# Layer 0 attention: band addition, row maximum and negation in one VectorE instruction, exponential in place in SBUF

## The chip, the core and the metric

The kernel runs on one core of a Trainium2 chip. The metric is the time of one execution on the device in microseconds (us); lower is better. The engines are named as in the profile: PE (TensorE matmul), PEld (its weight load), DVE (VectorE), ACT (ScalarE), POOL (GpSimd) and SP (the engine that issues most DMAs). SBUF is the on-chip memory, PSUM the accumulator memory with 8 banks of 128 x 512 fp32.

## What is computed

A chain of four transformer-like layers on x of shape 8 x 512 x 128. Only the attention of Layer 0 is touched. It has 16 heads of 8 channels and a relative-position bias with two parts (content to position, position to content). Per head the scores are a 512 x 512 matrix: a product of query and key, plus bias terms that depend on a bucket of the distance between query and key (equal beyond 64 positions), then a softmax along each row, then a product with the values:

```
scores = (q @ k.T + c2p[bucket(i - j)] + p2c[bucket(j - i)]) * 1/sqrt(24)
probs  = softmax(scores, axis=-1)
out    = probs @ v          # then output projection, residual, layer norm
```

## The kernel before

Layer 0 has 8 batches x 16 heads = 128 heads (NBH), each cut into 4 blocks of 128 queries. A block, v = 4 * head + block, is one step: 128 partitions (queries) x 512 columns (keys). Every engine runs its own instruction stream, written out by hand as a loop over steps u; semaphores order the engines. The own bands and "frames" of the bias near the diagonal come back from DRAM (`scr`): `g_out` (DVE) sums them into GG, SP writes GG out (`write(n)`) and reads it back shifted (`read(n)`, into CD, three buffers).

One step goes through these stations:

- PE `scores(v)` (`l0_pe`, matmuls at L577 and L580) fills PSUM bank v % 3. It waits until the exponential of v - 3 has read that bank: `pe.wait_ge(s_ex, v - 2)`.
- DVE `add(v)` (L181) adds the block's own band, 192 or 256 columns wide, from CW to the scores in PSUM. CW has two buffers of 960 columns, one per head, filled by POOL's `own_band(n)` with two products of 192 and 768 columns.
- DVE `most(v)` (L193) takes the negated maximum of each row of 512 into MX. In every second step `g_out` stands between `add` and `most`.
- ACT `exp(v)` (L167) reads PSUM, adds MX and writes the exponential to the probability buffer PB[v % 3]. It waits for `t_mm`, the transposes of v - 3.
- PE `p_tr(v)` (L335) transposes the four 128x128 pieces of PB, in loop step u = v + 4, after `scores(u)`.
- ACT `p_out(v)` (L171) copies the transposed block to SBUF, and PE `pv` (L157, 128*9) multiplies it with the values, in 4 of 16 steps.
- POOL also runs `corr` (two products of 512 columns a head, for g_out), `split` (6 instructions a batch, bf16 parts of q and k) and `tail` (3 instructions a batch). `small_mm` on PE are the projections and transposes of a batch, at steps listed in AHEAD and ENDS.

The order of the work on each engine is the order of these loops; nothing is scheduled by a planner. XR (512 columns) holds the difference in a split, T1 (4 x 128) the attention output of the batch before; `ct_out` on ACT writes T1 under its name CTT.

Of the kernel before, what the change touches and what calls it, by code (L numbers as in the profile page):

```python
# [8 lines left out]
ACT = mybir.ActivationFunctionType  # L9
# [195 lines left out]

def newton(dv, y, v, tmp):

    dv.step(dv.e.reciprocal(y, tmp))
    dv.settle()
    dv.step(tt(dv, tmp, y, y, ALU.mult))  # L210
    dv.settle()
    dv.step(tt(dv, tmp, tmp, v, ALU.mult))
    dv.settle()
    dv.step(ts(dv, tmp, tmp, -0.5, 1.5, ALU.mult, ALU.add))
    dv.settle()
    return tt(dv, y, y, tmp, ALU.mult)
# [11 lines left out]
def program(nc, a, out):  # L228
    ctx = ExitStack()
    with ctx:  # L230
# [133 lines left out]
        CW = [A0.take(960) for _ in range(2)]  # L364
# [4 lines left out]
        PBN = 3  # L369
# [7 lines left out]
        XR = A0.take(512)  # L377
        CTT = flat(T1)
# [34 lines left out]
        TMP0 = (XR, flat(T1), CT[:, :, :, :, :].rearrange("p a b c d -> p (a b c d)"))  # L413
# [6 lines left out]
        PGO_0, GG_0, VA_0, HALF_0 = 1, 3, 5, 6  # L420
        sgn, set_mm, set_dv, set_ac, sel_ok, pg_w, pg_r = (sem("set_" + k) for k in ("sgn", "mm", "dv", "ac", "sel", "pgw", "pgr"))
        s_mm, s_ad, s_mx, s_ex, t_mm, to_a = (sem("l0_" + k) for k in ("s_mm", "s_ad", "s_mx", "s_ex", "t_mm", "to_a"))
# [21 lines left out]
        ENDS = [{"heads": 17, "ct": 19, "mo": 29, "sw": 31, "stats": (34, 36, 38, 40), "var": 42, "root": 42, "scale": 46,  # L444
# [35 lines left out]
        def l0_pe(pe):  # L480
# [67 lines left out]
            def scores(v):  # L548

                n, ib = divmod(v, 4)  # L550
                G, hh = divmod(n, 4)
                (OQ, OL), OU = OP[G % OPN], OPU[G % 2]
                S = PS[:, v % 3, :]
                loaded(pe, G)
                loaded_u(pe, G)
                if v >= 3:
                    pe.wait_ge(s_ex, v - 2)
                pe.wait_ge(rd[n % 3], 16 * (n // 3 + 1))
                q = OQ[:, hh, ib * 128:ib * 128 + 128]
                band(S[:, 128 * ib:128 * ib + 128], frame(n, ib, 64, 192), ident, True)  # L560
                if ib == 0:
                    band(S[:, 128:256], frame(n, 1, -64, 64), ident, False)
                elif ib == 3:
                    band(S[:, 256:384], frame(n, 2, 192, 320), ident, False)
                else:
                    beside = S[:, 128 * ib - 64:128 * ib]
                    band(strided(beside, (192, 2), (1, 64)), frame(n, ib - 1, 192, 320), halves_swapped, False)
                far_step = 128 * ib + 64
                add(S[:, 0:far_step], q, OL[:, hh, 0:far_step], True)
                add(S[:, far_step:512], q, OU[:, hh, far_step:512], True).then_inc(s_mm, 1)  # L570
# [75 lines left out]
        def l0_dv(dv):  # L646
# [96 lines left out]
            def add(v):  # L743
                n, ib = divmod(v, 4)
                S = PS[:, v % 3, :]
                lo, hi = max(0, 128 * ib - 64), min(512, 128 * ib + 192)
                at = 256 * ib - 64 if ib else 0
                dv.wait_ge(s_mm, v + 1)
                dv.wait_ge(p_w, 2 * n + 2)
                tt(dv, S[:, lo:hi], S[:, lo:hi], CW[n % 2][:, at:at + hi - lo], ALU.add).then_inc(s_ad, 1)  # L750

            def most(v):
                dv.wait_ge(s_ad, v + 1)
                if v >= 8:
                    dv.wait_ge(s_ex, v - 7)
                minus_max(dv, MX[:, v % 8:v % 8 + 1], PS[:, v % 3, :]).then_inc(s_mx, 1)
# [56 lines left out]
            for u in range(STEPS0 + 1):  # L813
                n, ib = divmod(u, 4)
                b, r = divmod(u, 64)
                if 0 <= u - 1 < 4 * NBH:
                    add(u - 1)
                if u - 1 in G_AT:
                    g_out(*G_AT[u - 1])
                if 0 <= u - 1 < 4 * NBH:  # L820
                    most(u - 1)
# [13 lines left out]
        def l0_ac(ac):  # L835
# [46 lines left out]
            def exp(v):  # L882
                ac.wait_ge(s_mx, v + 1)
                if v >= PBN:
                    ac.wait_ge(t_mm, v - PBN + 1)
                act(ac, PB[v % PBN], PS[:, v % 3, :], ACT.Exp, bias=MX[:, v % 8:v % 8 + 1]).then_inc(s_ex, 1)

# [13 lines left out]
            def ct_out(b):  # L901
                ac.wait_ge(m_mm, number["ct", b, 0] + 1)
                ac.wait_ge(t1_ok, b)
                copy(ac, CTT, PS[:, B_M, :]).then_inc(m_ac, 1)

# [53 lines left out]
        def l0_po(po):  # L959
# [7 lines left out]
            def split(b, k, half):  # L967
# [4 lines left out]
                po.wait_ge(sp_p, 6 * b + 2 * k + half)  # L972
                if half == 0:
# [13 lines left out]
            def own_band(n):  # L987

                C, W = CD[n % 3], CW[n % 2]
                po.wait_ge(rd[n % 3], 16 * (n // 3 + 1))  # L990
                if n >= 2:
                    po.wait_ge(s_ad, 4 * (n - 1))
                tt(po, W[:, 0:192], C[:, 0:192], window[:, 64:256], ALU.mult).then_inc(p_w, 1)
                tt(po, W[:, 192:960].rearrange("p (f c) -> p f c", f=3), strided(C[:, 64:192], (128, 3), (1, 256)),
                   bc(window.unsqueeze(1), [128, 3, 256]), ALU.mult).then_inc(p_w, 1)
# [13 lines left out]
            ts(po, XN[:, 7, :], X[:, 7, :], NT0["mv"][:, 7, 0:1], NT0["y"][:, 7:8], ALU.subtract, ALU.mult).then_inc(n_xp, 4)  # L1009
            po.wait_ge(ld[0], 9 * 16)  # L1010
# [4 lines left out]
            own_band(0)  # L1015
            for u in range(STEPS0 + 1):
                n, ib = divmod(u, 4)
                b, r = divmod(u, 64)
                if ib == 2 and n + 1 < NBH:
                    own_band(n + 1)  # L1020
# [1937 lines left out]
```

## Time and profile before

| | |
|---|---|
| three runs, us | 2080.17, 2075.82, 2078.79 (median 2078.79) |
| span of the profiled execution, us | 2079.5 |
| PE, DVE, ACT, POOL busy over the span | 91%, 80%, 72%, 59% |
| stretch of Layer 0 at an even pace | about 100 to 800 us |

The span runs from the first to the last instruction of the profiled execution; what lies outside it is not shown, and the span falls among the three runs. Busy shares of engines overlap one another. "A <- B" in the waits means that A stood idle until B's instruction ended. A line such as L181 is that of a helper and is shared by many uses, so groups are told apart by tiles and shapes: AR is the large SBUF arena in which nearly all buffers lie, PS is PSUM, XN holds two of the three CD buffers.

### The profile page before, as it was taken

How to read it: one execution, taken by the hardware profiler on the slowest of the kernel's cores; microseconds unless marked ns; L12 is line 12 of the kernel's file. 1: busy time of each engine (PE TensorE's matmuls, PEld its weight loads, DVE VectorE, ACT ScalarE, POOL GpSimd, SP SyncE). 2: the span in 40 equal slices, each digit the busy share in tenths (PEclk: the TensorE clock that was granted, in tenths of full speed). 3: DMA queues.
4: the chain of work that ended last, by engine and by line, in shares of the span. 5: the costliest groups of instructions: out<-in, count | busy, mean ns of one | idle time of the engine just before them, and what ended most of it. 6: DMA issues, size and time to landing. Idle time of an engine off the chain costs nothing.

```text
span 2079.5 us, 38853 instructions
## 1 busy us (share of the span) xinstructions
PE 1901.5 (91%) x13494; PEld 1465.0 (70%) x13494; DVE 1670.8 (80%) x3871; ACT 1492.8 (72%) x2979; POOL 1217.4 (59%) x1026
## 2 busy tenths in 40 slices
PE   4899999999999999588997999999999888889998
PEld 3677676767777766454695888888887666668797
DVE  7798989999999999367088888888988787764686
ACT  5788888887888888244376677777777677776675
POOL 3878888887878875158064555555555544437300
PEclk7999999999999999699999999999999999999999
DMA  6999898988989885200000000000001000012000
GB/s 189 323 309 323 296 320 291 321 294 308 314 309 321 300 306 193 92 1 22 19 2 6 1 1 1 1 1 1 1 1 32 1 1 1 1 41 82 11 1 41
DMA packets 72264, 263.99 MB, mean 127 GB/s; under 512 B 10822, under 2 KB 30406, under 8 KB 71558
## 3 DMA queue, kind: packets, MB, share of 16 engines
q1 hardware_dynamic: 71126, 256.53, 36.3%
q10 hardware_dynamic: 944, 4.98, 0.6%
q8 instruction: 108, 1.77, 0.4%
q14 instruction: 86, 0.70, 0.1%
HBM read 140.17 MB, written 121.31 MB: 126 GB/s over the span
## 4 chain that ended last, share of the span: by engine, by line
PE 41%; DVE 7%; ACT 6%; POOL 2%; issue 2%; DVEq 0%; POOLq 0%; ACTq 0%
PE PS L157 10%; PE PS L335 8%; PE PS L161 8%; PE PS L163 7%; PE PS L162 7%; ACT AR L167 3%; ACT L167 2%; DVE AR L185 1%; DVE PT L181 1%; DVE DR L181 1%; ACT PT L171 1%; DVE AR L193 1%; POOL AR L176 1%; DVE AR L176 1%; DVE AR L181 0%
## 5 line engine op out<-in xcount | busy, mean ns | idle before, releaser
L167 ACT ACTIVATE AR<-PS,AR 128x512 f32<-128x512 f32 x1024 | 698.5, 690 | 204.0 <-DVE AR L193 91.4
L193 DVE TENSOR_REDUCE AR<-PS 128x1 f32<-128x512 f32 x896 | 615.4, 687 | 91.6 <-PE PS L163 76.0
L335 PE MATMUL PS<-ident,AR 128*128 128x128 f32 x3816 | 582.2, 277 | 32.5 <-DVE PT L181 18.5
L335 PEld LDWEIGHTS PS<-ident,AR 128*128 128x128 f32 x3816 | 444.8, 142 | 127.9 <-issue 45.6
L157 PE MATMUL PS<-AR 128*128 128x128 bf16 (+7 forms) x4126 | 484.8, 357 | 40.0 <-DVE AR L1379 14.6
L181 POOL TENSOR_TENSOR AR<-AR 128x512 f32<-128x512 f32 (+6 forms) x325 | 389.8, 1218 | 199.0 <-DVE AR L181 84.2
L176 POOL TENSOR_SCALAR AR<-AR 128x512 f32<-128x512 f32 (+1 forms) x146 | 256.0, 1754 | 265.6 <-DVE AR L1783 196.4
L171 ACT ACTIVATE AR<-PS 128x512 f32<-128x512 f32 (+3 forms) x596 | 348.5, 587 | 50.9 <-PE PS L157 27.2
L157 PEld LDWEIGHTS PS<-AR 128*128 128x128 bf16 (+4 forms) x4126 | 291.6, 131 | 114.7 <-issue 61.6
L171 ACT ACTIVATE PT<-PS 128x512 fp32r<-128x512 f32 x320 | 191.4, 598 | 161.2 <-PE PS L335 128.7
L181 DVE TENSOR_TENSOR AR<-PS,AR 128x512 f32<-128x512 f32 (+3 forms) x321 | 211.6, 660 | 70.0 <-PE PS L157 61.7
L181 POOL TENSOR_TENSOR AR<-XN,AR 128x192 f32<-128x192 f32 (+1 forms) x170 | 202.1, 1211 | 41.4 <-DMA XN<-scr 34.2
L181 DVE TENSOR_TENSOR PT<-PS,PT 128x512 fp32r<-128x512 f32 x320 | 217.3, 679 | 8.5 <-ACT PT L171 8.5
L181 DVE TENSOR_TENSOR PS<-PS,AR 128x192 f32<-128x192 f32 (+1 forms) x512 | 200.2, 391 | 23.1 <-PE PS L580 20.4
L580 PE MATMUL PS<-AR 128*128 128x448 bf16 (+4 forms) x1088 | 208.0, 274 | 0.0
L181 POOL TENSOR_TENSOR AR<-AR,XN 128x512 f32<-128x512 f32 x144 | 154.6, 1077 | 50.0 <-DVE AR L181 40.4
L577 PE MATMUL PS<-ident,XN 128*128 128x128 f32 x680 | 140.3, 288 | 19.0 <-ACT AR L167 16.8
L577 PEld LDWEIGHTS PS<-ident,XN 128*128 128x128 f32 x680 | 72.8, 143 | 108.5 <-issue 69.7
L161 PE MATMUL PS<-MH,XNr 128*128 128x512 f32 x256 | 122.5, 479 | 0.9 <-ACT AR L167 0.9
L580 PEld LDWEIGHTS PS<-AR 128*128 128x128 bf16 (+1 forms) x1088 | 110.6, 104 | 6.1
L167 ACT ACTIVATE AR<-AR 128x64 f32<-128x64 f32 (+6 forms) x168 | 88.5, 532 | 28.9 <-DVE AR L176 18.2
L161 PE MATMUL PS<-PT,VW 128*128 128x512 f32 x256 | 102.0, 399 | 0.0
(175 smaller groups left out, 2982.4 us busy)
## 6 DMA issues: line engine op xcount, KB each, us to landing
scr<-AR SPq DMA_DIRECT2D x128, 800.0 KB, 4.4
XN<-scr SPq DMA_DIRECT2D x85, 768.0 KB, 6.6
AR<-scr SPq DMA_DIRECT2D x43, 768.0 KB, 6.7
AR<-qsc SPq DMA_DIRECT2D x96, 192.0 KB
qsc<-AR SPq DMA_DIRECT2D x16, 384.0 KB, 4.1
qsc<-AR SPq DMA_DIRECT2D x16, 256.0 KB, 4.6
AR<-in_wgu SPq DMA_DIRECT2D x16, 256.0 KB, 3.2
qsc<-AR SPq DMA_DIRECT2D x16, 128.0 KB, 4.5
```

Source lines behind the costliest of these rows:

```text
L157: return pe.e.matmul(out, lhsT, rhs, start=start, stop=stop)
L161: pe.e.matmul(out, l[0], r[0], start=start, stop=False)
L162: pe.e.matmul(out, l[1], r[0], start=False, stop=False)
L163: return pe.e.matmul(out, l[0], r[1], start=False, stop=stop)
L167: return ac.e.activation(out, in_, func, bias=bias, scale=scale, accum_out=accum)
L171: return ac.e.activation(out, in_, ACT.Copy, bias=0.0, scale=1.0)
L176: return en.e.tensor_scalar(out, in0, s1, None, op0)
L181: return en.e.tensor_tensor(out, in0, in1, op)
L193: return dv.e.tensor_reduce(out, in_, AX.X, ALU.max, negate=True)
L335: return pe.e.transpose(out, in_, ident[0:k, 0:k])
L577: pe.e.matmul(out, lhsT, rhs, start=start, stop=start, is_transpose=True, skip_group_check=True)
L580: return pe.e.matmul(out, lhsT, rhs, start=False, stop=stop, skip_group_check=True)
```

## The change

The two DVE instructions `add` and `most` become `least(v)`: one fused instruction that adds the scores in PSUM and a 512-column slice of CW, multiplies by -1, writes the result to SBUF (PB[v % 4]) and keeps the running minimum, which a second 128x1 instruction writes to MX. CW is now one tile of 2240 columns that is zero outside the bands, so that each slice of 512 holds the block's band in its place: the end blocks (0 and 3) have two places, by n % 2, the middle blocks (1 and 2) one place for all heads. POOL's `own_band` becomes `own_ends` (2 x 192 columns, at the old place) and `own_middle` (2 x 256 columns, two steps later), and a memset of CW is added at the start. The exponential works in place in SBUF with scale -1. PB has four buffers instead of three. `scores(v)` waits for `s_mx`, the fused instruction of v - 3, instead of `s_ex`; the wait for the transposes moves from ACT to DVE. XR is dropped: splits use T1, `ct` moves from step 19 to 23 of a batch, and waits on `sp_p` and `t1_ok` guard T1.

```diff
+def add_least(dv, out, in0, in1, least):
+    return dv.e.tensor_tensor_reduce(out, in0, in1, -1.0, 3.0e38, ALU.add, ALU.min, least)
...
-        CW = [A0.take(960) for _ in range(2)]
+        CW = A0.take(2240)
+        CW_ENDS, CW_MID = (0, 1536), (768, 1216)
...
-        PBN = 3
+        PBN = 4
...
-        XR = A0.take(512)
-        CTT = flat(T1)
+        XR = CTT = flat(T1)
...
-        ENDS = [{"heads": 17, "ct": 19, "mo": 29, "sw": 31, "stats": (34, 36, 38, 40), "var": 42, "root": 42, "scale": 46,
+        ENDS = [{"heads": 17, "ct": 23, "mo": 29, "sw": 31, "stats": (34, 36, 38, 40), "var": 42, "root": 42, "scale": 46,
...
                 if v >= 3:
-                    pe.wait_ge(s_ex, v - 2)
+                    pe.wait_ge(s_mx, v - 2)
...
-            def add(v):
+            def least(v):
+
                 n, ib = divmod(v, 4)
                 S = PS[:, v % 3, :]
-                lo, hi = max(0, 128 * ib - 64), min(512, 128 * ib + 192)
-                at = 256 * ib - 64 if ib else 0
+                ends = CW_ENDS[n % 2]
+                at = (ends, CW_MID[0] - 64, CW_MID[1] - 192, ends + 192)[ib]
                 dv.wait_ge(s_mm, v + 1)
-                dv.wait_ge(p_w, 2 * n + 2)
-                tt(dv, S[:, lo:hi], S[:, lo:hi], CW[n % 2][:, at:at + hi - lo], ALU.add).then_inc(s_ad, 1)
-
-            def most(v):
-                dv.wait_ge(s_ad, v + 1)
+                dv.wait_ge(p_w, 2 * n + (2 if ib in (1, 2) else 1))
                 if v >= 8:
                     dv.wait_ge(s_ex, v - 7)
-                minus_max(dv, MX[:, v % 8:v % 8 + 1], PS[:, v % 3, :]).then_inc(s_mx, 1)
+                if v >= PBN:
+                    dv.wait_ge(t_mm, v - PBN + 1)
+                add_least(dv, PB[v % PBN], S, CW[:, at:at + 512], MX[:, v % 8:v % 8 + 1]).then_inc(s_mx, 1)
...
                 if 0 <= u - 1 < 4 * NBH:
-                    add(u - 1)
+                    least(u - 1)
                 if u - 1 in G_AT:
                     g_out(*G_AT[u - 1])
-                if 0 <= u - 1 < 4 * NBH:
-                    most(u - 1)
...
                 ac.wait_ge(s_mx, v + 1)
-                if v >= PBN:
-                    ac.wait_ge(t_mm, v - PBN + 1)
-                act(ac, PB[v % PBN], PS[:, v % 3, :], ACT.Exp, bias=MX[:, v % 8:v % 8 + 1]).then_inc(s_ex, 1)
+                act(ac, PB[v % PBN], PB[v % PBN], ACT.Exp, bias=MX[:, v % 8:v % 8 + 1], scale=-1.0).then_inc(s_ex, 1)
...
                 ac.wait_ge(t1_ok, b)
+                ac.wait_ge(sp_p, 6 * min(b + 3, NB))
...
                 po.wait_ge(sp_p, 6 * b + 2 * k + half)
+                po.wait_ge(t1_ok, max(0, b - 2))
...
-            def own_band(n):
-
-                C, W = CD[n % 3], CW[n % 2]
+            def own_ends(n):
+
+                C, at = CD[n % 3], CW_ENDS[n % 2]
                 po.wait_ge(rd[n % 3], 16 * (n // 3 + 1))
+                po.wait_ge(po_init, CW_0)
                 if n >= 2:
-                    po.wait_ge(s_ad, 4 * (n - 1))
-                tt(po, W[:, 0:192], C[:, 0:192], window[:, 64:256], ALU.mult).then_inc(p_w, 1)
-                tt(po, W[:, 192:960].rearrange("p (f c) -> p f c", f=3), strided(C[:, 64:192], (128, 3), (1, 256)),
-                   bc(window.unsqueeze(1), [128, 3, 256]), ALU.mult).then_inc(p_w, 1)
+                    po.wait_ge(s_mx, 4 * (n - 1))
+                tt(po, strided(CW[:, at:at + 192], (512, 2), (1, 192)), strided(C[:, 0:192], (320, 2), (1, 192)),
+                   strided(window[:, 64:256], (-64, 2), (1, 192)), ALU.mult).then_inc(p_w, 1)
+
+            def own_middle(n):
+
+                C = CD[n % 3]
+                if n >= 1:
+                    po.wait_ge(s_mx, 4 * n - 1)
+                tt(po, strided(CW[:, CW_MID[0]:CW_MID[0] + 256], (CW_MID[1] - CW_MID[0], 2), (1, 256)),
+                   strided(C[:, 64:320], (128, 2), (1, 256)), bc(window.unsqueeze(1), [128, 2, 256]), ALU.mult).then_inc(p_w, 1)
...
+            po.e.memset(CW, 0.0).then_inc(po_init, 1)
...
                 if ib == 2 and n + 1 < NBH:
-                    own_band(n + 1)
+                    own_ends(n + 1)
+                if ib == 0 and 1 <= n < NBH:
+                    own_middle(n)
```

On DVE, in the middle of Layer 0, two steps with a g_out in each, before (L181 with PS on the left is the band addition, L181 with AR on the left is g_out, L193 the maximum):

```order
L181 TENSOR_TENSOR AR<-PS,AR 128x2x2x128
L193 TENSOR_REDUCE AR<-PS 128x1
L181 TENSOR_TENSOR PS<-PS,AR 128x192
L193 TENSOR_REDUCE AR<-PS 128x1
L181 TENSOR_TENSOR PS<-PS,AR 128x192
L181 TENSOR_TENSOR AR<-PS,AR 128x512
L193 TENSOR_REDUCE AR<-PS 128x1
L181 TENSOR_TENSOR PS<-PS,AR 128x256
```

and the same place after (L207 is the fused instruction and, as 128x1, the write of its minimum):

```order
L181 TENSOR_TENSOR AR<-PS,AR 128x2x2x128
L207 ISA AR<-PS,AR 128x512
L207 ISA AR 128x1
L207 ISA AR<-PS,AR 128x512
L207 ISA AR 128x1
L181 TENSOR_TENSOR AR<-PS,AR 128x512
L207 ISA AR<-PS,AR 128x512
L207 ISA AR 128x1
```

Each step keeps two DVE instructions, one of them now 128x1 in place of 128x192 or 128x256, and g_out stands behind the pair instead of inside it.

On POOL, three heads of Layer 0 before, with the semaphores that each waits for (128x512 is corr, rd0 to rd2 are the reads from DRAM):

```order
L181 TENSOR_TENSOR AR<-AR 128x192 [waits l0_s_ad,l0_rd0]
L181 TENSOR_TENSOR AR<-AR 128x768
L181 TENSOR_TENSOR AR<-AR,XN 128x512 [waits l0_g_o,l0_m_ac]
L181 TENSOR_TENSOR AR<-AR,XN 128x512 [waits l0_g_o]
L181 TENSOR_TENSOR AR<-XN,AR 128x192 [waits l0_s_ad,l0_rd1]
L181 TENSOR_TENSOR AR<-XN,AR 128x768
L181 TENSOR_TENSOR AR<-AR,XN 128x512 [waits l0_g_o] x2
```

and after:

```order
L181 TENSOR_TENSOR AR<-XN,AR 128x2x192 [waits l0_s_mx,l0_rd1]
L181 TENSOR_TENSOR AR<-AR 128x512 [waits l0_g_o]
L181 TENSOR_TENSOR AR<-XN,AR 128x2x256 [waits l0_s_mx]
L181 TENSOR_TENSOR AR<-AR 128x512 [waits l0_g_o]
L181 TENSOR_TENSOR AR<-XN,AR 128x2x192 [waits l0_s_mx,l0_rd2]
```

The second band product stands one corr later and has a wait of its own.

## Rows read from the trace of the kernel before

**Rows 1.** Windows: length, busy PE, PEld, DVE, ACT, POOL, clock, DMA share, GB/s

```profile
100.00:800.00 700.00, 676.67 (x6015) 495.49 (x6014) 645.57 (x1363) 582.36 (x1043) 578.52 (x524) 1.00 0.90 308
536.36:560.03 23.67, 23.25 (x202) 16.46 (x200) 21.82 (x49) 20.78 (x38) 19.41 (x19) 1.00 0.89 299
560.03:584.86 24.83, 24.51 (x222) 18.07 (x220) 21.55 (x43) 21.54 (x41) 22.66 (x21) 1.00 0.99 346
584.86:609.54 24.68, 23.76 (x218) 17.96 (x216) 23.44 (x54) 19.06 (x34) 18.66 (x18) 1.00 0.87 299
609.54:633.67 24.13, 22.79 (x206) 16.71 (x204) 22.73 (x50) 20.38 (x38) 21.09 (x20) 1.00 0.88 294
```

**Rows 2.** Waits, whole run: us in total, times, longest

```profile
PEld PS L577 <- ACT AR L167: 55.5, 102, 2.3
...
PE PS L577 <- ACT AR L167: 24.2, 48, 1.4
```

**Rows 3.** Timeline of PE and of PEld: start, us, what

```profile
756.03 0.39 PE L157 MATMUL PS<-AR 128*128 128x128 bf16 x4
756.26 0.39 PE L577 MATMUL PS<-ident,XN 128*128 128x128 f32 x2
...
757.14 0.38 PE L577 MATMUL PS<-ident,XN 128*128 128x128 f32 x2
...
758.01 0.39 PE L157 MATMUL PS<-AR 128*128 128x128 bf16 x4
758.52 0.44 PE L577 MATMUL PS<-ident,XN 128*128 128x128 f32 x2
...
758.52 0.20 PEld L577 LDWEIGHTS PS<-ident,XN 128*128 128x128 f32 x2 [0.29 <-ACT AR L167]
```

**Rows 4.** Waits, 100 to 800 us

```profile
ACT AR L167 <- DVE AR L193: 78.7, 187, 1.2
...
ACT AR L167 <- PE PS L335: 37.1, 84, 0.7
```

**Rows 5.** Groups of DVE by form, whole run: busy us, mean ns | idle before

```profile
L193 DVE TENSOR_REDUCE AR<-PS 128x1 f32<-128x512 f32 x896 | 615.4, 687 | 91.6 <-PE PS L163 76.0
...
L181 DVE TENSOR_TENSOR AR<-PS,AR 128x512 f32<-128x512 f32 x280 | 192.2, 687 | 44.4 <-PE PS L157 37.2 <-POOL AR L181 5.4 <-DMA scr<-AR 1.0
L181 DVE TENSOR_TENSOR PS<-PS,AR 128x256 f32<-128x256 f32 x256 | 108.5, 424 | 4.6 <-PE PS L580 1.9
L181 DVE TENSOR_TENSOR PS<-PS,AR 128x192 f32<-128x192 f32 x256 | 91.7, 358 | 18.6 <-PE PS L580 18.5
...
L1783 DVE RECIPROCAL AR<-AR 128x1 f32<-128x1 f32 x256 | 39.1, 153 | 0.0
...
L1379 DVE TENSOR_TENSOR_SCAN AR<-AR 128x512 f32<-128x512 f32 x16 | 24.7, 1545 | 1.8 <-POOL AR L181 1.8
```

**Rows 6.** Groups of ACT by form, whole run

```profile
L167 ACT ACTIVATE AR<-PS,AR 128x512 f32<-128x512 f32 x1024 | 698.5, 690 | 204.0 <-DVE AR L193 91.4 <-PE PS L335 41.8 <-PE PS L157 36.7
...
L167 ACT ACTIVATE AR<-AR 128x512 f32<-128x512 f32 x16 | 11.8, 737 | 0.0
```

**Rows 7.** Groups of POOL by form, whole run

```profile
L181 POOL TENSOR_TENSOR AR<-XN,AR 128x768 f32<-128x768 f32 x85 | 155.2, 1826 | 0.0
...
L181 POOL TENSOR_TENSOR AR<-XN,AR 128x192 f32<-128x192 f32 x85 | 50.7, 596 | 41.4 <-DMA XN<-scr 34.2 <-DVE PS L181 6.2
...
L962 POOL MEMSET AR<- 128x1600 f32 x2 | 2.8, 1432 | 0.0
```

**Rows 8.** Timeline of POOL near the start

```profile
24.15 2.17 POOL L181 TENSOR_TENSOR AR<-AR 128x512 f32<-128x512 f32 x2 [11.70 <-ACT AR L171]
```

**Rows 9.** Waits, 560.03 to 584.86 us

```profile
PEld PS L577 <- ACT AR L167: 1.4, 2, 0.9
```

**Rows 10.** Line L1106 (the read from DRAM): who waited, time to landing

```profile
  POOL AR L181: 59.7, 49
...
DMA to landing us min/median/max: 4.3/6.7/10.4
```

More of the change, by code:

```diff
@@ L410, in program @@
         READ_AT.update({4 * n - 7: n for n in range(3, NBH)})
-        TMP0 = (XR, flat(T1), CT[:, :, :, :, :].rearrange("p a b c d -> p (a b c d)"))
+        TMP0 = (PB[3], flat(T1), CT[:, :, :, :, :].rearrange("p a b c d -> p (a b c d)"))
         SPLIT0 = {(0, 0): 1, (1, 0): 2, (0, 1): 3, (1, 1): 4, (2, 0): 5, (2, 1): 6}
@@ L419, in program @@
         PT_0, XN_0, PV_0 = 1, 2, 3
-        PGO_0, GG_0, VA_0, HALF_0 = 1, 3, 5, 6
+        PGO_0, GG_0, VA_0, HALF_0, CW_0 = 1, 3, 5, 6, 7
         sgn, set_mm, set_dv, set_ac, sel_ok, pg_w, pg_r = (sem("set_" + k) for k in ("sgn", "mm", "dv", "ac", "sel", "pgw", "pgr"))
-        s_mm, s_ad, s_mx, s_ex, t_mm, to_a = (sem("l0_" + k) for k in ("s_mm", "s_ad", "s_mx", "s_ex", "t_mm", "to_a"))
+        s_mm, s_mx, s_ex, t_mm, to_a = (sem("l0_" + k) for k in ("s_mm", "s_mx", "s_ex", "t_mm", "to_a"))
         g_mm, g_o, p_cr, p_w = (sem("l0_" + k) for k in ("g_mm", "g_o", "p_cr", "p_w"))
@@ L1014, in l0_po @@
             corr(2, 0)
-            own_band(0)
+            own_ends(0)
+            own_middle(0)
             for u in range(STEPS0 + 1):
```

## The prediction

> **What bounds the kernel now.** I read the windows first, because the change touches Layer 0 alone. Between 100 and 800 us PE is busy 676.67 of 700 us, DVE 645.57, ACT 582.36, POOL 578.52, and the DMA engines 0.90 of the time [rows 1]. The reader should see two engines near full at once: PE at 97% and DVE at 92%. The four rows under it are four pieces of one batch, 16 steps each, together 97.31 us, so a step takes 97.31 / 64 = 1.52 us and a head 6.08 us. In the second piece the DMA share is 0.99.
>
> Then the waits. In Layer 0 PE stands almost only at L577, the first matmul of a step's scores, which waits for the ACT exponential that frees its PSUM bank. L577 exists in Layer 0 only, so the list over the whole run gives it: 24.2 us as seen on PE, 55.5 us as seen on its weight loads [rows 2]. The two differ because a matmul's end is modelled. The timeline shows how: a whole step without extras runs from 757.14 to 758.01, 0.87 us; the four-matmul group at 758.01 is followed by L577 at 758.52, 0.51 us later, where the same group at 756.03 is followed after 0.23 us. PE shows no idle time at 758.52, yet 0.28 us is lost, and the weight-load row shows it as 0.29 us [rows 3]. So the true loss lies between the two numbers, above the first.
>
> Why is the exponential late? Between 100 and 800 us ACT itself waits 78.7 us for the row maximum (L193) and 37.1 us for the transposes (L335) that free a probability buffer [rows 4]. So the chain is scores, addition, maximum, exponential, next scores, with DVE its fullest link and no room to catch up.
>
> **The change part by part, durations from [rows 5].**
>
> *DVE.* Removed per head: two additions of 256 columns and two of 192, 2 x 424 + 2 x 358 = 1564 ns, and four maxima, 4 x 687 = 2748 ns. Added: four fused instructions and four 128x1 ones that write the result of the running minimum (the order shows them as pairs). The trace has no fused one. From below it costs what a plain 128x512 addition from PSUM and SBUF costs, 687 ns; from above, what the scan costs, the only row here that carries a value from one column to the next through two operations, 1545 ns. I take 687, because the maximum itself carries a value along the row and takes 687 as well, and the addition in front of it is a stage of the same stream. The 128x1 write lies between nothing and 358 ns (the smaller addition); I take the reciprocal of the same size, 153. A head: 4 x 840 + 2 x 687 (the g_out additions) = 4734 ns, against 1564 + 2748 + 1374 = 5686. That is 0.95 us less in every 6.08, 122 us over 128 heads. None of it is span by itself; at (645.57 - 115 heads x 0.95) / (700 - 28), it takes DVE from 92% to about 80% and off the chain.
> The Trainium skill (DVE: opcode table, instruction layouts, handler registers and perf-mode slots; section Datapath and trigger behaviour) says that a stage which reads its own previous result runs without a bubble, while the scan routes its value back to an earlier stage and runs at half throughput. By that rule the fused instruction has the price I take; by the scan's row without the rule, DVE would become the bound (third rival). The trace agrees as far as it goes: the maximum 687 ns, the scan 1545; no run here shows the fused form.
>
> *The bank.* The bank is free once the fused instruction has read it, not once the exponential has. From the end of the scores that is 840 ns instead of (391 + 687, and 687 more where g_out stands between) + 690. So L577's wait for ACT should vanish: 24.2 to 55.5 us. I take the middle, 40.
>
> *Four buffers.* The exponential waited for the transposes of v-3, which PE does only after the scores of v+1. Now the fused instruction of v waits for the transposes of v-4, which PE does straight after the scores of v: one group of four matmuls, less than the 0.87 us of a whole step [rows 3], behind the scores it waits for anyway. Behind it on DVE stand g_out and the next fused instruction; with DVE at 80% and the bank needed three steps later, this costs nothing. If DVE stayed at 92%, part of that would be lost in each step.
>
> *ACT.* The exponential reads SBUF: 737 ns against 690 [rows 6], 47 x 512 = 24 us on an engine that is idle for 117.6 of the 700. Hidden, except where ACT normalises in the same steps (4 steps in each of 8 batches): 32 x 0.05 = 1.5 us.
>
> *POOL.* Before 596 + 1826 = 2422 ns a head. The two rows give (1826 - 596) / 576 = 2.14 ns a column and 186 ns fixed, so 384 and 512 columns take 1006 and 1279, together 2285 [rows 7]: 0.14 us a head less, hidden under an engine that waits already. But the middle buffer is single: own_middle(n) can start only after block 2 of head n-1 and must end before block 1 of head n. That gap is three steps less one fused pair, 3 x 1.52 - 0.84 = 3.7 us on average and 3 x 0.87 + 0.23 - 0.84 = 2.0 in the shortest steps, for 1.28 us of work. Where POOL comes late (tail: 3 instructions, once a batch) I charge 0.2 us for each of 8 batches: 1.5 us. The new memset of 2240 columns, 1432 x 2240 / 1600 = 2.0 us, falls into POOL's 11.70 us of idle time before 24.15 [rows 7, 8].
>
> *T1 shared, "ct" at 23.* ct_out on ACT waits for POOL's last split, two steps earlier in its queue. Nothing if POOL keeps step; the next reader of T1 comes at step 29. I price it at zero; if POOL were late, exponentials queue behind it, about 1 us x 7.
>
> *What DMA takes back.* One batch needs 0.89 x 23.67 + 0.99 x 24.83 + 0.87 x 24.68 + 0.88 x 24.13 = 88.4 us of all 16 engines [rows 1]. PE's new pace is about 97.3 - 40/7.7 = 92.1 us a batch, a share of 0.96. On average it fits, but the second piece stands at 0.99 and cannot shrink. PE idles there for 24.83 - 24.51 = 0.3 us [rows 1] and its weight loads wait 1.4 us for ACT [rows 9]; the mean, 0.85, in 7 batches is 6 us that stay.
>
> *Sum.* 40 - 1.5 - 1.5 - 6 = 31 us. The profiled span is 2079.5 us, 0.7 above the median of the runs (2078.79), so I work on it as it stands: **2048.5 us**.
>
> **The rivals.**
> 1. *The wait comes back as another.* With DVE relieved, the band copy in front of it decides: data lands 6.7 us (10.4 at most) after its issue, and POOL already waits 59.7 us for it [rows 10]; with DMA at 0.96 it lands later, own_ends, a corr and own_middle follow in one queue, and the fused instruction waits. At 0.15 us a head it is 19 us: 2067. For: DMA is close to full. Against: the read is issued some eight steps ahead, 12 us at 1.52 us a step.
> 2. *No change*: POOL and DMA pace the short heads just as DVE did, all 31 us given back, 0.24 us a head: 2079. Against: POOL is idle for 121.5 of the 700 us [rows 1].
> 3. *Slower: the fused instruction runs like the scan.* 1545 + 153 = 1698 against 391 + 687 = 1078: 620 x 512 = 317 us more on DVE, which has 54.4 idle in 700, some 58 in all Layer 0. It ends at 2079.5 + 259 = 2338. It decides from a pair longer than 1078 + 58000/512 = 1190 ns. The Trainium skill's rule above speaks against it.
> 4. *More*: the whole 55.5 less DMA's 6: 2030.
>
> **How the numbers follow.** Forecast (18 to 45 us off) 0.70, first rival 0.14, no change 0.06, slower 0.07, more 0.03. About 0.2% (4 us) is what a measurement of this kernel tells from no change. The low end takes the upper bound of the waits less DMA's part and a little of the rest: 55.5 - 8 = 47.5, 2032. The high end takes the lower bound, 24.2 - 9 = 15, 2064, and reaches into the first rival: 2070. Faster 0.86, same 0.06, slower 0.08.
>
> **What the profile after would show.** DVE in Layer 0 near 80% busy; a 128x512 fused row near 690 ns and a 128x1 row near 150; L577's wait for ACT gone from PE and its weight loads; the four pieces of a batch near 22.8, 24.7, 23.7 and 22.3 us; DMA share 0.93 to 0.95; exponential near 740 ns. Wrong if the fused row is above 1.1 us, if DVE waits for POOL more than a few us in all, or if L577 waits for DMA or for DVE's fused instruction.

## The result, and the profile after

The changed kernel takes 2045.66 us (median of four runs, 2044.11 to 2048.12), the kernel before 2079.48 us (2075.82 to 2082.17) in the same comparison: ratio 0.9838, 95% interval 0.9824 to 0.9852. That is 33.8 us less; 31 were forecast, and 2048.5 us. Four executions in all the comparisons took far longer than the rest (2494.58, 3751.78, 3991.28 and 6136.49 us, the second of them the profiled one of the kernel before with four buffers); the ratios leave them out, and no wait is read from that profile.

**Windows** (columns as in [rows 1]): first a long stretch of the changed kernel, 100 to 770 us, then the four pieces of the same batch as in [rows 1].

```profile
100.00:770.00 670.00, 662.07 (x6049) 496.38 (x6049) 493.65 (x1376) 601.76 (x1048) 565.70 (x526) 1.00 0.93 323
...
517.19:540.82 23.63, 23.63 (x206) 16.49 (x203) 15.65 (x43) 22.59 (x41) 20.53 (x20) 1.00 0.94 318
540.82:565.21 24.39, 24.39 (x229) 19.31 (x229) 16.41 (x44) 21.45 (x38) 19.62 (x19) 1.00 0.97 349
565.21:588.17 22.96, 22.79 (x213) 17.23 (x211) 19.24 (x57) 20.41 (x35) 18.84 (x19) 1.00 0.92 312
588.17:610.35 22.18, 21.47 (x198) 16.06 (x199) 17.41 (x52) 19.61 (x37) 20.79 (x20) 1.00 0.94 315
```

The same stretch of the kernel before, which serves all comparisons below:

```profile
100.00:770.00 670.00, 647.59 (x5754) 474.45 (x5753) 617.70 (x1306) 559.06 (x1003) 556.43 (x504) 1.00 0.90 308
```

Read the counts first: in the same 670 us PE gets through 6049 matmuls instead of 5754, 5% more. DVE fell from 92% busy to 74%. PE was 96.7% busy and is now 98.8%: it is the fullest engine. That it alone sets the pace does not follow: further down, more work on DVE still costs time. The batch takes 93.16 us instead of 97.31.

**Groups** of DVE, ACT and POOL that answer to [rows 5], [rows 6] and [rows 7] (whole run, by form):

```profile
L207 DVE CUSTOM_DVE_ANT_0 AR<-PS,AR 128x512 f32<-128x512 f32 x512 | 349.6, 685 | 194.8 <-PE PS L339 155.9 <-POOL AR L181 18.5 <-ACT AR L167 10.9
...
L207 DVE DVE_READ_ACCUMULATOR2_ANT AR<- 128x1 f32 x512 | 42.3, 83 | 0.0
...
L167 ACT ACTIVATE AR<-AR 128x512 f32<-128x512 f32 x528 | 381.0, 722 | 47.3 <-DVE AR L207 46.3
...
L181 POOL TENSOR_TENSOR AR<-XN,AR 128x512 f32<-128x512 f32 x85 | 108.9, 1281 | 29.2 <-DVE AR L207 29.0
L181 POOL TENSOR_TENSOR AR<-XN,AR 128x384 f32<-128x384 f32 x85 | 85.7, 1008 | 48.1 <-DMA XN<-scr 47.9
```

The fused instruction costs 685 ns, as much as the maximum alone did, and the write of its minimum 83. By these durations a pair is 768 ns where addition and maximum took 391 + 687 = 1078, 0.31 us less in each step, 159 us over 512 steps. But durations overlap, and what a step costs DVE is the time from start to start. The timeline of DVE shows it, before:

```profile
505.76 0.36 DVE L181 TENSOR_TENSOR PS<-PS,AR 128x192 f32<-128x192 f32 x1
506.15 0.69 DVE L193 TENSOR_REDUCE AR<-PS 128x1 f32<-128x512 f32 x1
506.76 0.28 DVE L779 BATCH_NORM_STATS2 AR<-AR 128x6 f32<-128x128 f32 x1
```

and after:

```profile
505.02 0.69 DVE L207 CUSTOM_DVE_ANT_0 AR<-PS,AR 128x512 f32<-128x512 f32 x1
505.63 0.08 DVE L207 DVE_READ_ACCUMULATOR2_ANT AR<- 128x1 f32 x1
505.63 0.69 DVE L181 TENSOR_TENSOR AR<-PS,AR 128x512 f32<-128x512 f32 x1
```

Here addition and maximum take 506.76 - 505.76 = 1.00 us, the pair 505.63 - 505.02 = 0.61: the next instruction starts together with the write of the minimum, so that write takes no time of its own.

**Waits**, 100 to 770 us, of the changed kernel:

```profile
DVE AR L207 <- PE PS L339: 142.4, 146, 1.8
PEld PS L583 <- issue: 92.8, 125, 0.9
ACT AR L167 <- DVE AR L207: 42.2, 129, 1.8
...
PEld PS L583 <- DVE AR L207: 18.0, 21, 0.9
...
DVE AR L207 <- POOL AR L181: 15.8, 13, 2.0
```

and of the kernel before, same stretch:

```profile
PEld PS L577 <- issue: 90.5, 116, 0.9
ACT AR L167 <- DVE AR L193: 74.4, 177, 1.2
...
PEld PS L577 <- ACT AR L167: 47.0, 87, 1.1
...
PE PS L577 <- ACT AR L167: 19.7, 40, 0.9
```

L583, L586, L339 and L1121 are the L577, L580, L335 and L1106 of before. On PE the wait of the first score matmul is gone from the list. The wait for the transposes has moved from ACT to DVE and looks large (142.4 us). DVE is the engine with time to spare, so the wait need not cost anything; how near it is to costing something shows with three buffers, below.

Where in the run the time went shows in the windows of the whole of Layer 0, from its first score matmul to its last (L577 before, L583 after). Before:

```profile
48.50:842.50 794.00, 756.83 (x6661) 551.15 (x6662) 712.66 (x1508) 650.08 (x1164) 635.98 (x575) 0.99 0.87 298
```

and after:

```profile
48.10:804.90 756.80, 736.11 (x6661) 547.90 (x6662) 541.74 (x1508) 667.55 (x1164) 619.11 (x575) 1.00 0.90 312
```

So Layer 0 itself is 37.2 us shorter, and the span 2079.5 - 2044.3 = 35.2. The 2 us between them cannot be told from nothing: what lies outside this stretch takes 1285.5 us before and 1287.5 after, and between 1282.4 and 1289.8 us in the variants below, none of which touches it.

DVE's busy time fell by 170.9 us, 0.33 in each of 512 steps. How much of the gain shows as idle time of PE? PE issues the same 6661 matmuls in both. Its busy time falls from 756.8 to 736.1 us and its idle time from 37.2 to 20.7. More than half of the gain, 20.7 of 37.2 us, was never shown as idle: the same matmuls are just shown as less busy. The Trainium skill (Perfetto Trace Analysis; section Tensor Engine Instruction (MATMUL, LD_WEIGHTS)) says that the profiler estimates a matmul's end from its size instead of observing it; this trace fits that, with those 20.7 us of busy time lost by the same work, but does not prove it.

### The profile page after: what moved, and what is told of

It reads as the page before. It is cut to its first block, busy times and chain, and to the rows that moved or that the text cites. A ratio compares the mean times of both kernels' runs of the same rounds, so it can differ in the third digit from the quotient of the medians.

```text
span 2044.3 us, 38978 instructions
## 1 busy us (share of the span) xinstructions
PE 1882.9 (92%) x13494; PEld 1463.8 (72%) x13494; DVE 1503.8 (74%) x3871; ACT 1509.1 (74%) x2979; POOL 1199.4 (59%) x1027
## 4 chain that ended last, share of the span: by engine, by line
PE 42%; DVE 7%; ACT 6%; POOL 2%; issue 2%; DVEq 0%; ACTq 0%; POOLq 0%
PE PS L157 10%; PE PS L339 8%; PE PS L161 8%; PE PS L163 8%; PE PS L162 7%; ACT AR L167 3%; ACT L167 2%; DVE AR L185 1%; DVE DR L181 1%; DVE PT L181 1%; ACT PT L171 1%; POOL AR L176 1%; DVE AR L176 1%; DVE AR L193 0%; DVE AR L181 0%
## 5 line engine op out<-in xcount | busy, mean ns | idle before, releaser
L339 PE MATMUL PS<-ident,AR 128*128 128x128 f32 x3816 | 577.9, 276 | 39.8 <-DVE PT L181 17.9
L339 PEld LDWEIGHTS PS<-ident,AR 128*128 128x128 f32 x3816 | 447.1, 142 | 133.1 <-issue 49.6
L157 PE MATMUL PS<-AR 128*128 128x128 bf16 (+7 forms) x4126 | 484.8, 357 | 41.1 <-DVE AR L1394 14.9
L167 ACT ACTIVATE AR<-AR 128x512 f32<-128x512 f32 (+3 forms) x680 | 455.2, 674 | 76.9 <-DVE AR L207 46.3
L207 DVE CUSTOM_DVE_ANT_0 AR<-PS,AR 128x512 f32<-128x512 f32 x512 | 349.6, 685 | 194.8 <-PE PS L339 155.9
L181 POOL TENSOR_TENSOR AR<-AR 128x512 f32<-128x512 f32 (+7 forms) x325 | 386.0, 1201 | 181.9 <-DVE AR L181 66.5
L176 POOL TENSOR_SCALAR AR<-AR 128x512 f32<-128x512 f32 (+1 forms) x146 | 251.9, 1726 | 268.6 <-DVE AR L1798 200.3
L167 ACT ACTIVATE AR<-PS,AR 128x512 f32<-128x512 f32 x512 | 346.4, 688 | 77.7 <-PE PS L157 38.6
L157 PEld LDWEIGHTS PS<-AR 128*128 128x128 bf16 (+4 forms) x4126 | 291.8, 131 | 116.1 <-issue 64.6
L193 DVE TENSOR_REDUCE AR<-PS 128x1 f32<-128x512 f32 x384 | 263.6, 687 | 82.3 <-PE PS L163 75.7
L181 POOL TENSOR_TENSOR AR<-XN,AR 128x384 f32<-128x384 f32 (+1 forms) x170 | 194.5, 1144 | 77.4 <-DMA XN<-scr 47.9
L181 DVE TENSOR_TENSOR AR<-PS,AR 128x512 f32<-128x512 f32 (+3 forms) x321 | 211.2, 658 | 38.1 <-PE PS L157 31.0
L181 DVE TENSOR_TENSOR PT<-PS,PT 128x512 fp32r<-128x512 f32 x320 | 216.8, 678 | 8.5 <-ACT PT L171 8.5
L586 PE MATMUL PS<-AR 128*128 128x448 bf16 (+4 forms) x1088 | 207.0, 273 | 0.0
L181 POOL TENSOR_TENSOR AR<-AR,XN 128x512 f32<-128x512 f32 x144 | 154.9, 1076 | 10.9 <-ACT AR L167 7.0
L583 PE MATMUL PS<-ident,XN 128*128 128x128 f32 x680 | 135.9, 282 | 0.9 <-DMA XN<-scr 0.9
L583 PEld LDWEIGHTS PS<-ident,XN 128*128 128x128 f32 x680 | 73.6, 142 | 79.7 <-issue 64.9
L586 PEld LDWEIGHTS PS<-AR 128*128 128x128 bf16 (+1 forms) x1088 | 110.1, 104 | 5.9
```

What stands on the lines that cost most here:

```text
L157: return pe.e.matmul(out, lhsT, rhs, start=start, stop=stop)
L167: return ac.e.activation(out, in_, func, bias=bias, scale=scale, accum_out=accum)
L176: return en.e.tensor_scalar(out, in0, s1, None, op0)
L181: return en.e.tensor_tensor(out, in0, in1, op)
L193: return dv.e.tensor_reduce(out, in_, AX.X, ALU.max, negate=True)
L207: return dv.e.tensor_tensor_reduce(out, in0, in1, -1.0, 3.0e38, ALU.add, ALU.min, least)
```

## The experiments

Each expectation letters its theories for itself; after it I name them by what they say. Differences "over after" are the ratio less 0.9838, times 2078.8 us; a ratio's interval is some 0.0015 to each side, so 3 us or less is not told apart.

### What the release of the bank is worth

```diff
-                    pe.wait_ge(s_mx, v - 2)
+                    pe.wait_ge(s_ex, v - 2)
```

> The changed kernel with one wait put back: the scores of v wait for the exponential of v-3 (s_ex) and not for the fused instruction. Theory A (my forecast: the earlier release of the PSUM bank is what pays): the release comes 722 ns later in every step, PE waits for ACT at its band transposes again, and a good part of the 34 us goes: 2055 to 2070 us. Theory B (the relief of DVE pays, and the bank would have been free in time anyway): at most 3 us over the changed kernel, 2045 to 2049 us. I lean to something between, 2053 us, since the chain is still shorter than before: 685 + 83 + 722 = 1490 ns against 391 + 687 + 690 = 1768, and 2455 where g_out stood between.

Measured 2042.32 us, ratio 0.9833 (0.9818 to 0.9847): the bank held until the exponential, as before, costs nothing, and my own guess between the two theories, 2053, was wrong. The windows of this kernel, 100 to 770 us, and under them a row of its waits there:

```profile
100.00:770.00 670.00, 662.93 (x6057) 497.42 (x6056) 495.23 (x1378) 603.38 (x1050) 564.71 (x526) 1.00 0.93 323
```

```profile
PEld PS L583 <- ACT AR L167: 102.0, 127, 0.9
```

A wait of 102.0 us for ACT stands in the list of a kernel that is as fast. The reader should compare it with the 92.8 us put down to "issue" in the changed kernel: nearly all of it is the same idle time under another name. The timeline of the changed kernel shows what it is, first on PE, then on PE's weight loads:

```profile
505.29 1.04 PE L157 MATMUL PS<-AR 128*9 128x512 f32 x8
506.26 0.44 PE L583 MATMUL PS<-ident,AR 128*128 128x128 f32 x2
```

```profile
505.28 0.12 PEld L157 LDWEIGHTS PS<-AR 128*9 128x9 f32 x8 [0.17 <-issue]
506.26 0.20 PEld L583 LDWEIGHTS PS<-ident,AR 128*128 128x128 f32 x2 [0.86 <-DVE AR L207]
```

The eight weight loads of `pv` are done early and its matmuls fill PE until 506.26; the next weight load stands idle 0.86 us beside a PE that works. The idle time of weight loads is thus no upper bound for what PE loses, which is how I had used it.

### Without the fusion

Addition from PSUM to SBUF, then the maximum from SBUF, with the early release, the four buffers and everything else of the change (only the exponential loses its scale of -1, since the addition does not negate):

```diff
-                add_least(dv, PB[v % PBN], S, CW[:, at:at + 512], MX[:, v % 8:v % 8 + 1]).then_inc(s_mx, 1)
+                tt(dv, PB[v % PBN], S, CW[:, at:at + 512], ALU.add).then_inc(s_ad, 1)
+                dv.wait_ge(s_ad, v + 1)
+                minus_max(dv, MX[:, v % 8:v % 8 + 1], PB[v % PBN]).then_inc(s_mx, 1)
...
-                    pe.wait_ge(s_mx, v - 2)
+                    pe.wait_ge(s_ad, v - 2)
```

> The changed kernel with the fused instruction taken apart: a 128x512 addition from PSUM into the probability buffer, then the negated maximum from SBUF; the bank is released after the addition, so earlier than in the changed kernel. Theory A (only the bank's release matters): 2044 to 2050 us, as the changed kernel. Theory B (DVE must be relieved as well): DVE has 6 instructions of 128x512 a head that start 0.60 us apart, plus about 0.6 us a head of other work: 6 x 1.0 x 0.60 x (10 per head in all: 4 additions, 4 maxima, 2 g_out) = 6.0, so 6.6 us a head against 5.83 now, near 0.77 x 128 = 100 us more: about 2145 us, with DVE above 97% busy in Layer 0.

Measured 2183.65 us, ratio 1.0516 (1.0500 to 1.0531), 39 us more than expected. DVE's busy time was close to the estimate (856.9 us in Layer 0, 6.7 a head, for 6.6), but a head took 7.0 us. The windows, 100 to 770 us, and then the first of the waits there:

```profile
100.00:770.00 670.00, 601.26 (x5109) 411.79 (x5107) 654.14 (x1147) 520.48 (x892) 483.93 (x447) 1.00 0.82 275
```

```profile
ACT AR L167 <- DVE AR L193: 137.7, 247, 1.3
```

DVE is 98% busy and PE falls to 90%. The bank is released even earlier than in the changed kernel, and with a DVE as full as this that does not help. Without the fusion the rest of the change is a loss of 5%.

### The fourth buffer

```diff
-        PBN = 4
-        PB = [A0.take(512) for _ in range(PBN)]
+        PBN = 3
+        PB = [A0.take(512) for _ in range(4)]
```

> The changed kernel with three probability buffers in use instead of four: the fused instruction of v waits for the transposes of v-3, which PE does after the scores of v+1. Theory A (the fourth buffer is needed because the wait now stands on DVE, ahead of the bank's release): the release comes one step later, PE waits for DVE at its band transposes: 2052 to 2065 us. Theory B (as I priced it, the buffers' wait lies in the slack of DVE): within 3 us of the changed kernel.

Measured 2118.72 us, ratio 1.0206 (1.0189 to 1.0223): 76 us over after, and slower than before, far outside what either theory gave. The opposite edit, four buffers in the kernel before:

```diff
-        PBN = 3
+        PBN = 4
```

> The kernel before with four probability buffers instead of three and nothing else: its exponential waits for the transposes of v-4 instead of v-3. Theory A (the buffers are part of the gain: ACT waited 37 us for these transposes, and they lie in the chain that makes the exponential late): 2060 to 2070 us, 6 to 15 us less than before. Theory B (DVE at 92% is the link, and the fourth buffer only pays for the wait that the change moves to DVE): within 4 us of the kernel before.

Measured 2078.72 us, ratio 0.9999 (0.9989 to 1.0009): nothing. The changed kernel with three buffers, 100 to 770 us, windows and then waits:

```profile
100.00:770.00 670.00, 629.70 (x5544) 451.75 (x5542) 463.12 (x1260) 550.72 (x967) 525.14 (x486) 1.00 0.88 297
```

```profile
DVE AR L207 <- PE PS L339: 184.8, 320, 1.3
ACT AR L167 <- DVE AR L207: 117.1, 200, 1.2
...
PEld PS L583 <- DVE AR L207: 87.4, 102, 0.9
```

No engine is full (PE 94%, DVE 69%): this is a chain. The timeline of DVE shows each fused instruction waiting for the transposes (L339):

```profile
504.33 0.69 DVE L207 CUSTOM_DVE_ANT_0 AR<-PS,AR 128x512 f32<-128x512 f32 x1 [0.70 <-PE PS L339]
...
505.47 0.69 DVE L207 CUSTOM_DVE_ANT_0 AR<-PS,AR 128x512 f32<-128x512 f32 x1 [0.44 <-PE PS L339]
...
506.08 0.69 DVE L181 TENSOR_TENSOR AR<-PS,AR 128x512 f32<-128x512 f32 x1
...
507.47 0.69 DVE L207 CUSTOM_DVE_ANT_0 AR<-PS,AR 128x512 f32<-128x512 f32 x1 [0.70 <-PE PS L339]
```

With three buffers the fused instruction of v needs the transposes of v - 3, which PE does at the end of step v + 1, and the scores of v + 3 need the fused instruction. One step lies between, 0.87 us where it is short, for a fused instruction of 0.69 us and in every second step a g_out ahead of it that takes 0.60 from start to start: 1.29. With four buffers the transposes come a step earlier and two short steps, 1.74 us, lie between. In the kernel before it was ACT that waited for the transposes, and DVE was free of them. That count of steps is my reading; what the runs show is that the buffer is needed where the wait stands on DVE, and worth nothing where it stands on ACT. A fifth buffer was not tried.

### How much DVE time counts

An addition of 128 columns from PSUM into a scratch tile, ahead of each fused instruction of the changed kernel:

```diff
+                dv.settle()
+                dv.step(tt(dv, JUNK, S[:, 0:128], CW[:, at:at + 128], ALU.add))
                 add_least(dv, PB[v % PBN], S, CW[:, at:at + 512], MX[:, v % 8:v % 8 + 1]).then_inc(s_mx, 1)
```

> The changed kernel with one more DVE instruction in each step, an addition of 128 columns from PSUM into an unused tile, ahead of the fused one. A 128-column addition took 292 ns, so a step's DVE work is 292 + 685 + 83 = 1060 ns, as much as the 391 + 687 = 1078 of the kernel before; buffers, order and waits stay as changed. Theory A (the relief of DVE is the gain): back to 2070 to 2085 us. Theory B (the shorter chain and the buffers are the gain, DVE may be as full as it was): 2045 to 2055 us.

Measured 2058.52 us, ratio 0.9913 (0.9891 to 0.9934): 16 us over after, between the two theories. The windows, 100 to 770 us, then the group of the dummy, then one step of the timeline of DVE:

```profile
100.00:770.00 670.00, 657.77 (x5921) 484.29 (x5920) 566.95 (x1796) 585.97 (x1028) 556.99 (x516) 1.00 0.92 317
```

```profile
L181 DVE TENSOR_TENSOR AR<-PS,AR 128x128 f32<-128x128 f32 x544 | 152.9, 286 | 122.0 <-PE PS L339 71.2 <-ACT AR L167 25.6 <-POOL AR L181 14.0
```

```profile
507.08 0.28 DVE L181 TENSOR_TENSOR AR<-PS,AR 128x128 f32<-128x128 f32 x1
507.28 0.68 DVE L207 CUSTOM_DVE_ANT_0 AR<-PS,AR 128x512 f32<-128x512 f32 x1
```

Added up by durations, as the expectation did it, the dummy of 286 ns gives back nearly all that the fusion saves (310 ns). The trace says otherwise: from start to start it takes 0.20 us, where the fusion took away 0.33 a step, and DVE is 85% busy, not 92%. The whole of Layer 0 gives the sizes:

```profile
48.00:820.50 772.50, 747.02 (x6662) 545.52 (x6663) 636.18 (x2020) 664.16 (x1164) 621.19 (x575) 1.00 0.89 306
```

DVE gets back 636.2 - 541.7 = 94.4 of the 170.9 us that the change took from it, 55%, and Layer 0 is 15.7 us longer, 42% of its gain. If the loss grew evenly, all of the DVE time given back would cost some three quarters of the gain. That is an estimate, and a run with all 170.9 us was not made. The dummy also stands ahead of the fused instruction and so delays the minimum; the run does not separate the two.

Could the early release of the bank count once DVE is fuller? Both edits together:

> Both edits together: scores wait for the exponential of three steps before (as in the kernel before) and VectorE has one more addition of 128 columns in each step (286 ns). The bank held alone cost nothing, the load alone some 15 us. Theory A (the early release of the bank counts once VectorE is fuller): 10 us or more over the load alone, ratio above 0.996. Rival (the release never counts): within 4 us of the load alone, ratio 0.989 to 0.993.

Measured 2059.67 us, ratio 0.9912 (0.9897 to 0.9926), the same as the load alone. The release does not count here either, with DVE 85% busy; at the 92% of the kernel before it was not tried.

### The order on DVE

Is it that g_out no longer stands between addition and maximum? In the kernel before, the maximum straight behind the addition:

```diff
                 if 0 <= u - 1 < 4 * NBH:
                     add(u - 1)
+                    most(u - 1)
                 if u - 1 in G_AT:
                     g_out(*G_AT[u - 1])
-                if 0 <= u - 1 < 4 * NBH:
-                    most(u - 1)
```

> The kernel before, with the maximum straight behind the band addition and g_out behind both on VectorE, no fusion, three buffers; VectorE does the same work, only its order changes. Theory A (what the changed kernel gains is VectorE's time, 0.31 us a step; the order is worth nothing while VectorE is at 92%): within 5 us of before, 2074 to 2084. Rival (half of the gain or more comes from g_out no longer standing between addition and maximum, which delayed each second exponential by 0.69 us): 2050 to 2062.

Measured 2075.78 us, ratio 0.9985 (0.9975 to 0.9994): 3 us of the 34, just distinguishable. This is not the order alone, though. The whole of Layer 0 in this run:

```profile
47.90:837.70 789.80, 754.21 (x6661) 550.26 (x6662) 723.85 (x1508) 647.94 (x1164) 634.89 (x575) 0.99 0.87 299
```

DVE is busy 723.9 us for 712.7 before, with the same instructions: 11.2 us of its time went into the new order, and the 3 us are what is left after that. Then g_out ahead of the fused instruction in the changed kernel:

```diff
-                if 0 <= u - 1 < 4 * NBH:
-                    least(u - 1)
                 if u - 1 in G_AT:
                     g_out(*G_AT[u - 1])
+                if 0 <= u - 1 < 4 * NBH:
+                    least(u - 1)
```

> The changed kernel with g_out ahead of the fused instruction in each step that has one, so that the maximum is 0.69 us later there, as it was in the kernel before; VectorE does the same work. Theory A (only VectorE's busy time counts; the bank is needed three steps later): within 5 us of the changed kernel, ratio to before 0.982 to 0.986. Rival (the latency of the maximum counts): 15 to 30 us over the changed kernel, ratio 0.991 to 0.998.

Measured 2060.44 us, ratio 0.9914 (0.9898 to 0.9930): 16 us over after, although DVE does no more work. The theory that only DVE's busy time counts falls. Windows, 100 to 770 us, and then waits:

```profile
100.00:770.00 670.00, 657.36 (x5911) 484.64 (x5909) 482.02 (x1340) 575.65 (x1027) 552.60 (x514) 1.00 0.92 316
```

```profile
DVE AR L181 <- PE PS L157: 165.9, 175, 1.8
PEld PS L583 <- DVE AR L207: 95.9, 112, 0.9
ACT AR L167 <- DVE AR L207: 94.6, 162, 1.4
```

DVE is 72% busy, but now it stands in g_out waiting for a matmul (L157) while scores that are ready lie behind it, and the exponential waits 94.6 us instead of 42.2. So this order costs 16 us at equal DVE work (540.7 us busy in Layer 0 for 541.7). The two runs are no mirror images: in the kernel before, g_out stood between addition and maximum, here it stands ahead of both. What the old order would cost the changed kernel is therefore not known, and the two numbers, 3 and 16, do not add up to a share of the gain.

### What else could hold the changed kernel back

POOL's `tail` delays own_middle; two steps later it would not stand in its way:

```diff
-                 "norm": (47, 48, 49, 50), "sum": 51, "last": (58, 58, 60, 60), "lastvar": 62}] * NB
+                 "norm": (47, 48, 49, 50), "sum": 53, "last": (58, 58, 60, 60), "lastvar": 62}] * NB
```

> The changed kernel with POOL's tail (three products and sums a batch) two steps later, behind own_middle instead of in front of it (sum: 53 for 51). Theory A (what is left of the first rival: the single middle buffer makes DVE wait 1.8 us for POOL once a batch, and PE 0.9 us for DVE): these waits go, 0.4 to 0.9 us in 7 batches, 2039 to 2043 us. Theory B (PE makes it up elsewhere, or POOL is then late for own_ends): no change, 2044 to 2048 us.

Measured 2042.18 us, ratio 0.9831 (0.9817 to 0.9846): 1.5 us less than after, not told apart, although the waits of DVE for POOL in this window go from 15.8 us to 0.5. And DMA, with part of the data left out (the last 512 of 1600 columns of GG are not written for the later heads, so their bias is partly stale):

```diff
-                sp.e.dma_start(bass.AP(scr.tensor, n % SLOTS * 128 * ROW, [[ROW, 128], [1, ROW]]), GG[n % 2]).then_inc(wr[n % 2], 16)
+                W = ROW if n < SLOTS else ROW - 512
+                sp.e.dma_start(bass.AP(scr.tensor, n % SLOTS * 128 * ROW, [[ROW, 128], [1, W]]), GG[n % 2][:, 0:W]).then_inc(wr[n % 2], 16)
```

> The changed kernel, whose write of GG to DRAM leaves out the last 512 of its 1600 columns for all heads but the first few, so that the bias of the later heads is partly stale: 256 of some 1570 KB a head less on the DMA engines, share in Layer 0 from 0.93 to about 0.80. Theory A (PE at 98.8% sets the pace and the DMA engines take nothing back): within 4 us of the changed kernel, ratio 0.982 to 0.986. Rival (the DMA engines are what kept it from more, as my prediction charged 6 us for it): 5 to 10 us faster, ratio 0.979 to 0.981.

Measured 2043.51 us, ratio 0.9828 (0.9813 to 0.9843), 2 us under after and not told apart, with the DMA engines clearly relieved (0.83 instead of 0.93):

```profile
100.00:770.00 670.00, 663.70 (x6061) 497.68 (x6059) 495.64 (x1383) 603.73 (x1052) 566.80 (x526) 1.00 0.83 278
```

Last, PE itself: the 128x128 matmuls of g_out's product doubled, first in the changed kernel, then in the kernel before. A group of four of them takes 0.22 us (in the timeline the score matmul at 756.26 follows one that began at 756.03 [rows 3]), and there are 256 groups: 56 us of PE work.

```diff
-                for q in range(4):
+                for q in (0, 1, 2, 3, 0, 1, 2, 3):
```

> The changed kernel with the four matmuls of g_of issued twice (256 groups, same result): 0.22 us each between starts, 56 us of PE work in all. Theory A (PE now sets the pace of Layer 0 alone): 50 to 56 us more, 2095 to 2101 us. Theory B (DMA at 0.93 or POOL shares the pace): 25 to 40 us more, since part of the added work falls into waits.

> The kernel before with the same doubled g_of group, 56 us of PE work. Theory A (in the kernel before PE waited for a chain through DVE, and the added work fits partly into those waits): 25 to 40 us more than before. Theory B (PE was the bound before as well): 50 to 56 us more.

Measured 2090.77 us after (ratio 1.0060, 1.0044 to 1.0076), 46 us over the changed kernel, and 2112.15 us before (ratio 1.0160, 1.0142 to 1.0178), 33 us over the kernel before. The kernel before falls into its first range; the changed one falls between its two, so PE sets most of its pace and not all. The changed kernel absorbs 10 of the 56 us, the kernel before 23: it had more idle time on PE to put them in. The windows, after and then before:

```profile
100.00:770.00 670.00, 668.74 (x6552) 516.58 (x6551) 478.34 (x1290) 573.86 (x989) 536.78 (x498) 1.00 0.89 304
```

```profile
100.00:770.00 670.00, 660.21 (x6375) 503.33 (x6374) 590.05 (x1258) 539.77 (x964) 536.08 (x486) 1.00 0.87 296
```

No kernel tried here is faster than the changed one by more than a measurement tells.

## Why the prediction was right, and where it was not

Forecast 31 us, measured 33.8. The path was as forecast in the main: DVE is relieved and PE waits less. The sum is closer than its terms deserve. By its steps:

- **DVE.** Fused instruction 685 ns for 687, write of the minimum 83 for 153, so 768 ns for 840, and DVE at 74% for "about 80%". The prediction added durations, which overlap: from start to start the pair takes 0.61 us, and DVE was relieved of 170.9 us where 122 were forecast. The bound taken from the maximum was right and the scan's (1543 ns here) was not; the trace agrees with the rule quoted there from the Trainium skill (DVE: opcode table, instruction layouts, handler registers and perf-mode slots; section Datapath and trigger behaviour).
- **The bank.** "So L577's wait for ACT should vanish: 24.2 to 55.5 us. I take the middle, 40." The size was near (Layer 0 became 37.2 us shorter), the reason given was wrong. Holding the bank until the exponential costs nothing (held_bank), with a DVE at 85% neither (held_and_loaded). What is left as the reason is that the fused instruction, and with it the exponential, comes earlier. The upper bound was no bound: weight-load idle time holds the 0.86 us beside a `pv` that costs nothing. The middle of two numbers, one of them no bound, came out near by luck.
- **Four buffers.** "This costs nothing" held. That the fourth buffer would be worth 76 us when absent the prediction did not see; it named a DVE at 92% as the danger, and the danger was one buffer less.
- **ACT and POOL.** Exponential 722 ns for 737, products 1008 and 1281 ns for 1006 and 1279. DVE waits 18.5 us in all for POOL, 2.0 at the longest, where 1.5 us of cost were charged; moving the tail away gives 1.5 us, not told apart from nothing. By its own sign of being wrong, "if DVE waits for POOL more than a few us in all", the prediction would be wrong; the sign was too strict, since nearly all of that wait went in tail_late and no more than a few us with it. The 1.5 us charged to ACT were not tested by themselves, nor was T1 shared by two uses.
- **What DMA takes back.** This is the term that failed: "the second piece stands at 0.99 and cannot shrink", "6 us that stay". It shrank from 24.83 to 24.39 us, at 0.97, with PE busy through all of it and 229 matmuls in it for 222; it has the most of the four. With a tenth of the DMA share taken away the kernel gains 2 us or nothing.
- **The sum.** The four pieces were 23.6, 24.4, 23.0 and 22.2 us for 22.8, 24.7, 23.7 and 22.3. Without the 6 us charged to DMA the sum would give 37, and Layer 0 gained 37.2; that agreement rests on the 40 above, and is luck as well.
- **The rivals.** The band copy lands later than before (median 7.0 us, 11.2 at most, against 6.7 and 10.4 [rows 10]), and the reads hold POOL up 68.2 us instead of 59.7, but of this little reaches DVE (18.5 us of waits for POOL). One more sign of being wrong was met, "if L577 waits for DMA or for DVE's fused instruction": its weight loads wait 18.0 us for it. Those are weight loads beside a PE that is 98.8% busy. That the wait for ACT is gone from this line says little, since the line no longer waits for ACT by construction. "No change" and "slower" are excluded by the rows of DVE; "more" rested on the 55.5 us that were no bound.

Settled is that the fusion is necessary, that the fourth buffer is, and that the early release is not, at a DVE of up to 85%. Of the 34 us, 16 are lost when DVE gets back 55% of its time as work, and 16 when g_out goes ahead of the fused instruction. The runs do not divide the gain further; that both act through the same thing, how late the maximum comes, is my reading. Why the other order was worth only 3 us in the kernel before is in part the 11.2 us of DVE time that it took; the rest is argued, not shown: behind a DVE at 92% the next addition comes late anyway.

## What to carry to other kernels

When two engines are near full in one chain, take time from the one whose result the other waits for, and check with runs that add work to each: here 56 us more on PE cost 46 after and 33 before, and 94 us more on DVE cost 16 after, which tells how much slack was left. Price such a load, and what a fusion saves, from start to start or by the engine's busy time over the whole stage, not by durations: the dummy lasts 0.29 us and costs DVE 0.20. When a wait moves to another engine, count how many steps lie between what it waits for and who needs its result; a buffer that is worth nothing in the old order (0 us) can be worth more than the whole gain in the new one (76 us). Put the instruction that others wait for ahead of one that itself waits, even on an engine with a quarter of its time free (16 us here).

## What was not expected of the hardware

- The write of the fused instruction's result takes 83 ns, about half of the 153 of a reciprocal of the same 128x1 size, and it lies within the last of the fused instruction's own 0.69 us: in the timeline the next instruction starts 0.61 us after the fused one, together with the write.
- Addition, scaling, write-out and running minimum over 512 columns take as long as the plain maximum: 685 ns and 687.
- The exponential in place in SBUF takes 722 ns on average where the 16 instructions of that shape before took 737 [rows 6], and 690 from PSUM.
- PE's busy time fell by 20.7 us in Layer 0 with the same matmuls, which was more than its idle time fell (16.5 us).
